# Output weights and two output tiles loaded in the third pass, and row maxima transposed with 128 stationary columns behind a projection's piece

## What is computed

```python
q = (resid @ Wq).reshape(B, T, N_HEADS, D_HEAD).transpose(0, 2, 1, 3)
k = (resid @ Wk)...; v = (resid @ Wv)...
q = q * cos + _rotate_half(q) * sin
k = k * cos + _rotate_half(k) * sin
att = jnp.einsum('bhgqd,bhkd->bhgqk', qg, k) / math.sqrt(D_HEAD)
att = jnp.where(causal[None, None, None], att, -jnp.inf)
probs = jax.nn.softmax(att, axis=-1)
ctx = jnp.einsum('bhgqk,bhkd->bhgqd', probs, v)
out = ctx @ Wo
x = x + attention(layernorm(x))
x = x + (silu(xt @ W_gate.T) * (xt @ W_up.T)) @ W_down.T      # xt = layernorm(x)
```

## Time and profile before

| | us |
|---|---|
| median of 3 runs | 801.76 (801.19 to 802.27) |
| the profiled execution | 802.57 |
| its span, first to last instruction | 800.9 |
| TensorE busy in the span | 760.1 (95%) |
| VectorE, ScalarE, GpSimd busy | 444.1, 343.6, 211.5 |
| mean granted TensorE clock | 0.983 of full speed |

### The profile page before, as it was taken

How to read it: one execution, slowest core, us unless ns; L and a number is a source line. 1 busy time by engine, 2 the same in 40 slices (tenths; PEclk the granted TensorE clock), 3 DMA queues, 4 the chain that set the end, 5 groups by cost and what they waited for, 6 DMA issues and landing times.

```text
span 800.9 us, 12101 instructions
## 1 busy us (share of the span) xinstructions
PE 760.1 (95%) x4193; PEld 506.5 (63%) x4224; DVE 444.1 (55%) x1000; ACT 343.6 (43%) x684; POOL 211.5 (26%) x384
## 2 busy tenths in 40 slices
PE   4689999999999998999799999999999999999998
PEld 3525454544445443444487887888878888788886
DVE  7787888788877887897345543233322243241212
ACT  3417768767776776667543321111121111121111
POOL 3416764577436763234300000000000000000000
PEclk9959999999999999899999999999999999999999
DMA  7346586234333326470287100502004120030001
GB/s 262 99 99 234 185 268 207 69 101 120 107 86 94 113 81 205 121 210 31 89 233 204 50 27 33 151 28 79 27 1 165 45 79 26 0 106 0 1 1 52
DMA packets 74613, 81.84 MB, mean 102 GB/s; under 512 B 8720, under 2 KB 58384, under 8 KB 74352
## 3 DMA queue, kind: packets, MB, share of 16 engines
q1 hardware_dynamic: 74128, 80.77, 33.1%
q10 hardware_dynamic: 432, 0.39, 0.2%
HBM read 57.02 MB, written 33.36 MB: 113 GB/s over the span
## 4 chain that ended last, share of the span: by engine, by line
PE 81%; DVE 9%; SPq 3%; ACT 2%; DMA 2%; issue 1%; ACTq 0%; DVEq 0%
PE bank L1488 32%; PE ps_y L1540 14%; PE ps_o L1151 9%; PE ps_s L1106 8%; PE ps_t L1138 8%; PE ps_d L1058 6%; DVE ps_s L863 4%; PE ps_d L1079 1%; ACT probs L730 1%; PE ps_s L1111 1%; DVE m_parts L874 1%; SPq L426 1%; DVE xt_lo L842 1%; PE bank L1527 1%; SPq L173 1%
## 5 line engine op out<-in xcount | busy, mean ns | idle before, releaser
L730 ACT ACTIVATE probs<-ps_t 128x512 f32<-128x512 f32 (+1 forms) x352 | 185.7, 562 | 93.5 <-PE ps_t L1138 92.6
L863 DVE CUSTOM_DVE_ANT_0 ps_s<-ps_s,mask_row 128x512 f32<-128x512 f32 (+1 forms) x256 | 154.4, 644 | 33.8 <-PE ps_s L1106 33.6
L1445 DVE TENSOR_TENSOR h<-h,bank 128x512 f32<-128x512 f32 (+1 forms) x44 | 30.3, 688 | 215.7 <-PE bank L1488 214.6
L1106 PE MATMUL ps_s<-k_rows,q_rows 96*128 96x256 bf16 (+3 forms) x512 | 134.6, 316 | 10.8 <-DMA q_rows<-scratch_q_parts 5.0
L1138 PE MATMUL ps_t<-q_rows,k_rows 98*128 98x512 bf16 (+1 forms) x352 | 127.5, 366 | 6.9 <-DMA q_rows<-m_t 3.3
L1106 PEld LDWEIGHTS ps_s<-k_rows,q_rows 96*128 96x128 bf16 x512 | 44.0, 99 | 91.3 <-issue 33.6
L1383 ACT ACTIVATE h<-bank 128x512 f32<-128x512 f32 (+1 forms) x44 | 26.3, 599 | 149.4 <-PE bank L1488 149.3
L638 POOL TENSOR_SCALAR_AFFINE_SELECT probs<-probs 128x512 f32<-128x512 f32 x128 | 84.8, 662 | 0.0
L1151 PE MATMUL ps_o<-probs,v_ones 128*32 128x512 f32 (+3 forms) x1024 | 82.6, 441 | 0.2 <-ACT o_sb L740 0.2
L1389 ACT CAST h_hi<-h 128x512 fp32r<-128x512 f32 (+1 forms) x44 | 27.3, 621 | 125.5 <-DVE h L1445 125.5
L218 POOL TENSOR_TENSOR var_eps<-mean_var,eps 128x1 f32<-128x1 f32 x16 | 3.0, 190 | 290.0 <-DVE mean_var L213 290.0
(11 more groups left out here) (154 smaller groups left out, 1352.1 us busy)
## 6 DMA issues: line engine op xcount, KB each, us to landing
scratch_o<-o_sb SPq DMA_DIRECT2D x31, 256.0 KB, 2.3
q_rows<-scratch_q_parts SPq DMA_DIRECT2D x32, 192.0 KB
x_in<-in_x SPq DMA_DIRECT2D x16, 256.0 KB, 4.9
q_rows<-scratch_q_parts SPq DMA_DIRECT2D x32, 128.0 KB
x_res<-in_x SPq DMA_DIRECT2D x16, 256.0 KB, 2.7
o_in<-scratch_o SPq DMA_DIRECT2D x64, 64.0 KB
inverse<-scratch_inverse SPq DMA_DIRECT2D x64, 64.0 KB
out<-x_in SPq DMA_DIRECT2D x16, 256.0 KB, 2.1
```

The lines of the kernel that those rows point to most:

```text
L730: nc.scalar.activation(probs[:, g % 2, heads * u:heads * (u + 1), CHUNK_AT[c]:CHUNK_AT[c + 1]], ps_t[:, pos % S_BANKS, 0:heads * CHUNK_N[c ...
L863: nc.vector.tensor_tensor_reduce(out=bank, in0=bank, in1=mask_row[:, T - width:T], scale=1.0, scalar=LOWEST, op0=ALU.add, op1=ALU.max, acc ...
L1106: mm = nc.tensor.matmul(bank[:, place], q_rows[r][0:ROWS, j, P * q:P * (q + 1)], k_rows[r][0:ROWS, 0:width], start=(place == 0), stop=(hea ...
L1445: nc.vector.tensor_tensor(h[0:m, r], h[0:m, r], bank[units["up", f] % BANKS][0:m, :], ALU.mult).then_inc(h_ready, 1)
```

## The change

Three things are changed.

1. `prepare_batch_0` loses its slot 0. A new `prepare_first_tiles` runs in pass 2: the output weights in slot 18, output tile 0 with residual tile 0 in slot 22, output tile 1 with residual tile 1 in slot 26. It stands last in its slot, behind `store_o`.
2. `O_LOAD` goes from 0 to 2, and the function now loads only tiles 2 and 3: in slots 10 and 14 of pass 3, where slots 8 and 12 were.
3. `m_parts` gets 128 columns for each buffer (32 used, 96 cleared once at the start by a VectorE memset), so that `transposed_max` has 128 stationary columns and writes 128 rows. And `transposed_max` now stands behind the projection's piece in gap (0, 3), not ahead of it.

```diff
-WO_HI, WO_LO, O_LOAD, CTX_SCALE, CTX_HI, CTX_LO = 2, 4, 0, 5, 6, 7
+WO_HI, WO_LO, O_LOAD, CTX_SCALE, CTX_HI, CTX_LO = 2, 4, 2, 5, 6, 7
+WO_LOAD, FIRST_O_LOAD = 18, 22
...
-        m_parts = sb("m_parts", [P, 2, 2, GROUP, TT], BF16)
+        m_parts = sb("m_parts", [P, 2, P // (GROUP * TT), GROUP, TT], BF16)
...
-            def prepare_batch_0(slot):
-                if slot == 0:
+            def prepare_first_tiles(slot):
+
+                if slot == WO_LOAD:
                     sp.wait_ge(raw_copied, 13 * DMA)
                     sp.dma_start(to.wo[1][:].bitcast(F32), d["wo_raw"].rearrange("(c p) n -> p c n", p=P)
                                  ).then_inc(wo_loaded, DMA)
-                    load_residual(sp, d, to, 0, 0)
-                    load_residual(sp, d, to, 0, 1)
+                for t in range(2):
+                    if slot == FIRST_O_LOAD + TT * t:
+                        load_o(sp, d, to, 0, t)
+                        load_residual(sp, d, to, 0, t)
+
+            def prepare_batch_0(slot):
...
                 t = (slot - O_LOAD) // TT
-                if slot == O_LOAD + TT * t and t < TT:
-                    if t >= 2:
-                        sp.wait_ge(to.ctx_lo_ready, t - 1)
+                if slot == O_LOAD + TT * t and 2 <= t < TT:
+                    sp.wait_ge(to.ctx_lo_ready, t - 1)
                     load_o(sp, d, to, 0, t)
...
+                    if b == B - 2:
+                        prepare_first_tiles(slot)
                     if not has_next:
                         prepare_batch_0(slot)
...
+            nc.vector.memset(m_parts[:, :, 2:], 0.0)
...
-                nc.tensor.matmul(to[0:2 * GROUP * TT, 0:P], m_parts[:, n % 2].rearrange("p w j q -> p (w j q)"),
+                nc.tensor.matmul(to[:, 0:P], m_parts[:, n % 2].rearrange("p w j q -> p (w j q)"),
...
+                        for place, kind, k, piece in pieces.get((slot, j), ()):
+                            dense(b + 2 if has_next and kind == "T" else b + 1, kind, k, UNIT0[b] + place, piece)
                         if (i, j) == (0, GROUP - 1) and n + 1 < GROUPS:
                             transposed_max(n + 1)
-                        for place, kind, k, piece in pieces.get((slot, j), ()):
-                            dense(b + 2 if has_next and kind == "T" else b + 1, kind, k, UNIT0[b] + place, piece)
```

More of the change, by code:

```diff
@@ L1117, in transposed_max @@
                     bank_free(PRE_UNITS - 1, 0)
-                    to, ready = ps_d, dense_ready
+                    to, ready = ps_d[:], dense_ready
                 else:
```

## The result

The changed kernel takes 805.11 us (median of seven runs, 803.68 to 807.39) against 801.76 (seven runs, 800.58 to 802.78). The ratio is 1.0041, with a 95% interval of 1.0026 to 1.0056: slower by 3.35 us, where I had forecast 802.2 and a range of 797.5 to 805.0. The profiled execution took 807.39, 2.3 us above its median, and spans 805.7 us. The one of before was 0.8 above its own, so a difference of the two traces (4.8) is some 1.5 us too large.

The account below looks back on a forecast made before the run. TensorE, 81% of the span, was taken as the bound. Moved loads +3.5, slots 10 and 14 +0.2 and transposes -3.3 made +0.4 on the profiled 802.57, so 802.2 against the median 801.76; range 797.5 to 805.0.

Parts of the forecast that it names:

- stall at pass 2 slot 28: Rows for pass 2 slot 28 land late behind the slot 22 loads: new TensorE wait of 1.2 us, bounds 0.5 and 2.
- stall at pass 3 slot 0: Rows for pass 3 slot 0 land late behind the slot 26 loads: new wait of 4.3 us (3.5 to 5.2).
- half clock in slots 0 to 3: In pass 3, the clock falls after the new stall and costs 2.4 us, ends 0 and 3.0.
- slots 4 to 7: In pass 3, the old stall goes and the group takes 10.2 us, near VectorE's work; ends 9.7 and 11.3.
- from slot 24 of pass 2 to slot 8 of pass 3: Sum over the stretch 300.60 to 332.00: 31.4 us becomes 34.9, so +3.5; +1.1 if the clock stays up.
- slots 10 and 14, seen in slots 16 to 19: In pass 3, tile 3 issued behind the feed-forward weights, nearer its use: +0.2 us, at most 0.7.
- transposes: 128 stationary columns save 0.27 us in ten groups with a piece, 0.64 in four others: -3.3 us, bounds -1.2 and -4.1.
- part 1: Loads moved from pass 3 slots 0 and 4 into pass 2 slots 18, 22 and 26: +3.5 us by queue issue time.
- Part 2: The widened and moved transposes of the maxima, no longer differing in shape from neighbouring products: -3.3 us.
- the wait of 6.4 is no gain of its own: The transposes' 6.4 us wait for input lies where VectorE bounds one product later, so hiding it gains nothing.
- the stall-free case: Rival: the moved loads find room in the queue and the stall is gone: -7.5 us, 794.3; chance 0.13.
- "Slower": Rival: transposes give only 1.0 us while the moved loads cost their full 3.5: +2.7, 804.5; chance 0.25.

Follow-up runs that it names:

- e8_tile3_first: The changed kernel with the loads of output tile 3 put ahead of the feed-forward weights in pass 3 slot 14: 804.93 us.
- e3_tiles23_back: The changed kernel with output tiles 2 and 3 loaded in slots 8 and 12 of pass 3 again: 800.25 us.
- e1_transposes: The kernel before with only the transposes changed (128 stationary columns, behind the projection's piece): ratio 0.9936, 796.78 us without its one slow run.
- e2: The changed kernel with the transposes put back as they were, so only the loads moved: 808.26 us.
- e9: The changed kernel with output tile 1's eight loads in pass 2 slot 26 cut from 128 columns to 16, as many DMAs: 804.75 us.
- e10: The changed kernel with the feed-forward weights issued in slot 17 of pass 3, not slot 14; tile 3 stays in slot 14: 804.93 us.
- e7_tile1_early: The changed kernel with output tile 1 and its residual loaded in slots 5 and 6 of pass 2, not slot 26: 797.98 us.
- e4_room: The changed kernel with tiles 0 and 1 loaded in halves in slots 1, 2, 5, 6 of pass 2, tiles 2 and 3 in slots 8 and 12: 794.12 us.
- e5_wide_only: The kernel before with m_parts widened to 128 stationary columns, the transpose still ahead of the projection's piece: 799.09 us.
- e6_moved_only: The kernel before with the transpose moved behind the projection's piece, still with 32 stationary columns: 800.61 us.

## Why the prediction failed, step by step

| step | forecast | the change's trace |
|---|---|---|
| stall at pass 2 slot 28 | 1.2 | 1.9 |
| stall at pass 3 slot 0 | 4.3 | 4.9 |
| half clock in slots 0 to 3 | 2.4 | 2.2 |
| slots 4 to 7 | 10.2 | 9.8 |
| from slot 24 of pass 2 to slot 8 of pass 3 | +3.5 | +4.3 |
| slots 8 to 11 | 0 | +0.4 |
| slots 10 and 14, seen in slots 16 to 19 | +0.2 | +4.1 |
| transposes | -3.3 | -3.1 from pass 0 slot 4 to pass 2 slot 24, and 0.3 in each of two groups behind |

**The step that failed** is the paragraph on slots 10 and 14 of pass 3, "+0.2, at most 0.7". Its issue times were right: from 351.33 to 357.64 for ten loads, 6.3 for 6.2. Wrong was the landing, "2 to 3.5", taken from rows ahead of which no large load stood; behind 1.5 MB of weights it took 5.3, and with the tile ahead of the weights (e8_tile3_first) at most 3.6. VectorE was due for the tile at 359.55 (362.31 - 2.76), 8.2 after the first of these issues and not the 8.7 (7.5 + 1.2) of the forecast. The forecast's own worst case, 9.7 against 8.7, was besides 1.0 late and not 0.7. And I priced the lateness as if it came alone. It stands in VectorE's order ahead of maxima, so all of it reached TensorE, and a fall of the clock with it. e3_tiles23_back, the change without this step, runs at 800.25: inside the range, and 2 us under the forecast.

By medians the whole comes apart like this: the transposes -5.1 (e1_transposes at 796.78), part 1 on top of them +3.5 (e3_tiles23_back less e1_transposes), slots 10 and 14 on top of both +4.9 (the change less e3_tiles23_back). The forecast had -3.3, +3.5 and +0.2. Two terms were wrong in opposite directions. That the measured time lies only 0.1 us above the range is their cancelling, and luck.

**Part 1, slots 22 and 26**: mechanism, places and order right, and by medians the size too. In the trace of the change each term is short by 0.6 to 0.7, since the last row DMA reaches TensorE 4.2 us after its issue (308.61 to 312.79), not 3.5. But that is one execution: in e2, e3, e8, e9 and e10 it is 3.3 to 3.8, and in the four of them whose clock did not fall before that wait began, the wait at pass 3 slot 0 is 4.36 (e3), 4.48 (e8), 5.19 (e9) and 3.83 (e10), with the forecast's 4.3 among them. The queue's issue time as the cause is shown by e9_few_bytes. I left out that slots 8 to 11, without the stall, are 0.4 to 0.7 longer.

**The clock**: a fall was forecast and came, but its price is no constant. In the six kernels with the same two stalls (the change, e3, e9, e8, e10 and e2) the profiled executions have slots 0 to 3 at 10.56, 10.64, 10.21, 9.69, 9.21 and 8.40, by where the half speed begins and whether it lasts 6.8 or 3.4 us. In e7_tile1_early, with the 1.4 us wait alone, none came there. What decides the place stays open.

**Part 2**: the mechanism was right, the term too small. Alone the transposes give 5.1, not 3.3, and more than the bound of 4.1: 0.30 to 0.32 in a group and not 0.27, and about 15 such groups and not ten, with 0.64 in four others. That "the wait of 6.4 is no gain of its own" was wrong in part: the place alone took 0.10 off the gap, and 0.8 us off the kernel. Why a change between 32 and 128 stationary columns has a price is not shown; the runs show only the price.

The Trainium skill, "TensorE: Matmul & The Clock Gate", LDWEIGHTS, puts a weight load at P / 1.2 ns for P columns, which as an estimate is 27 ns for 32 columns and 107 for 128. The traces do not agree for 32 columns: they take 93 ns in the earlier trace rows, and 128 columns take 98 ns in the change:

```profile
L1130 PEld LDWEIGHTS ps_t<-ident_b,m_parts 128*128 128x128 bf16 x31 | 3.0, 98 | 9.4 <-issue 6.3 <-DVE m_parts L881 3.1
```

**The rivals**: the stall-free case, 794.3, was rightly given little here, but e4_room shows that it was to be had with tiles 0 and 1 some 56 to 61 us further ahead: 794.12. The Trainium skill, "DMA: Bandwidth & Descriptors", Rules for kernel authors, advises to issue a DMA early and wait late. Here that paid or not by the place in the queue: e3_tiles23_back and e4_room both load tiles 0 and 1 ahead of pass 3, at two places of one queue, and stand at 800.25 and 794.12. "Slower", 0.25, came true by a mechanism that was none of my rivals.

## What to carry to other kernels

A load moved earlier in a queue is not early, it is ahead of something: write down the queue's idle times between issues, and fit its issue time (here 5.7 us for nine DMAs) in them, in halves if need be. Then do the same for whatever is moved later, with the landing behind the largest transfer near it, and look which engine's order the late arrival stops. And when a load is turned around in such a queue, look for the next user that waits: here three orders gave about the same time with three different waits.

## What the runs showed of the hardware

- The issue of one DMA of a tile takes SyncE 0.6 us, with 64 KB (0.60) and with an eighth of it (0.60). A single one can take longer: 1.62 in e9_few_bytes, 1.45 in e5_wide_only, 1.43, 1.25 and 1.20 in e6_moved_only. What decides it is open.
- With a tile and 1.5 MB of weights directly ahead (e8_tile3_first) the next issue took 2.33 us, for a residual of 256 KB, elsewhere 0.46; behind the same weights alone it took 0.50 (e3_tiles23_back). From issue to use it was 5.3 us for the tile behind the weights, and 6.3 for the weights themselves.
- Between products of 128 stationary columns, one of 32 made the gap 0.35 us longer (0.92 to 1.27); one of 128 in the same place leaves it at 1.03, and behind the piece the next product starts 0.07 after it (280.48 to 280.55).
- In one trace each, slots 0 to 3 took 8.40 where the half clock fell ahead of another wait (e2_loads), and 2.2 us more where it fell into full work (the change).
